# Two-layer transformer on one core: the token lists of the experts found by counting in place of repeated maxima

## The reference, cut to what matters

```python
logits = xf @ router_w.T                       # T x 64
scores = softmax(logits)
topk_w, topk_idx = top_k(scores, 8)
topk_w = topk_w / (topk_w.sum(-1, keepdims=True) + 1e-20)
slot_expert = topk_idx.reshape(-1)
onehot = one_hot(slot_expert, 64)
pos = (cumsum(onehot, axis=0) * onehot).sum(-1) - 1
valid = pos < 128
dest = where(valid, slot_expert * 128 + pos, 64 * 128)
# xb[e, s] = the s-th token that chose expert e; zeros where there is none
hmid = silu(xb[e] @ w_gate[e]) * (xb[e] @ w_up[e])     # 512 -> 192
yb   = hmid @ w_down[e]                                # 192 -> 512
# out[token] += yb[e, s] * topk_w
# recurrence, per batch:
r, f, c = silu(xn @ Wr), sigmoid(xn @ Wf), silu(xn @ Wc)
h = associative_scan over 1024 times of h = f*h + (1-f)*c
y = r * rmsnorm(h, ln_scale) @ Wo
```

## Time and profile before

| | |
|---|---|
| time, median of 3 runs | 3461.34 us (3455.7 to 3472.47) |
| time of the profiled execution | 3456.27 us |
| its span | 3454.1 us |
| granted TensorE clock, mean | 0.960 of 2.4 GHz |
| PE busy | 3128.1 us, 91% |
| DVE busy | 1855.5 us, 54% |
| POOL busy | 1606.5 us, 47% |
| ACT busy | 1257.1 us, 36% |
| moved by DMA | 424.95 MB, mean 123 GB/s |

### The profile page before, as it was taken

One profiled execution on the slowest core, in us unless ns is written; L12 is line 12 of the kernel. 1 busy time (PEld: TensorE's weight loads), 2 busy tenths in 40 slices (PEclk: granted clock), 3 DMA queues, 4 the chain that ended last, 5 costly groups with the idle time before them and its releaser, 6 DMA issues. The chain is left out here.

```text
span 3454.1 us, 45609 instructions
## 1 busy us (share of the span) xinstructions
PE 3128.1 (91%) x16217; PEld 2440.1 (71%) x16217; DVE 1855.5 (54%) x3969; ACT 1257.1 (36%) x2827; POOL 1606.5 (47%) x1410
## 2 busy tenths in 40 slices
PE   5999999899999989999998999999858099999996
PEld 3777777777878777787877778787637067676764
DVE  5455556655555565555566555556528852434431
ACT  3344444334434333433333343343352023232322
POOL 2366657624554653455465244545511154444352
PEclk8999999999999999999999999999889599999998
DMA  6433223352223234211222421221073168787876
GB/s 211 157 114 105 97 89 104 131 170 99 89 86 108 89 106 156 86 62 68 80 87 91 154 73 62 80 92 50 22 251 119 36 181 225 205 213 205 220 206 141
DMA packets 219406, 424.95 MB, mean 123 GB/s; under 512 B 22448, under 2 KB 102960, under 8 KB 217136
## 3 DMA queue, kind: packets, MB, share of 16 engines
q1 hardware_dynamic: 200624, 377.99, 32.7%
q0 software_dynamic: 18560, 44.05, 6.8%
HBM read 311.22 MB, written 110.69 MB: 122 GB/s over the span
## 5 line engine op out<-in xcount | busy, mean ns | idle before, releaser
L776 POOL TENSOR_SCALAR probs<-probs,comb 128x512 f32<-128x512 f32 (+3 forms) x384 | 221.6, 586 | 1018.2 <-DVE comb L725 1018.0
L897 ACT ACTIVATE probs<-score_ps,neg_max 128x640 f32<-128x640 f32 (+7 forms) x512 | 374.4, 738 | 481.5 <-DVE neg_max L731 481.5
L731 DVE TENSOR_REDUCE neg_max<-score_ps 128x2 f32<-128x256 f32 (+7 forms) x256 | 347.2, 1356 | 114.4 <-PE score_ps L1025 113.4
L781 POOL TENSOR_TENSOR probs<-probs 128x512 f32<-128x512 f32 (+3 forms) x384 | 383.9, 1014 | 10.7
L785 POOL TENSOR_TENSOR out_root<-out_root,neg_half 128x16 f32<-128x16 f32 x128 | 372.5, 2911 | 4.8 <-DVE out_root L708 4.8
L820 ACT ACTIVATE attT<-turn_ps 128x512 fp32r<-128x512 f32 (+3 forms) x384 | 189.0, 492 | 470.6 <-PE turn_ps L934 468.3
L633 DVE TENSOR_TENSOR layer_sum<-product_ps,layer_sum 128x512 f32<-128x512 f32 x384 | 262.9, 685 | 30.8 <-PE product_ps L40 24.6
L1022 PE MATMUL score_ps<-keys_all,queries_all 64*128 64x512 f32 (+3 forms) x2304 | 278.0, 364 | 0.0
L620 DVE TENSOR_TENSOR attT<-turn_ps,attT 128x512 fp32r<-128x512 f32 (+3 forms) x384 | 212.7, 554 | 106.6 <-ACT attT L820 103.9
L678 DVE SCALAR_TENSOR_TENSOR hidden<-gate_tanh,product_ps 128x512 f32<-128x512 f32 x128 | 88.0, 688 | 312.7 <-ACT gate_tanh L862 312.7
L1022 PEld LDWEIGHTS score_ps<-keys_all,queries_all 64*128 64x128 f32 x2304 | 187.6, 186 | 67.4 <-issue 31.1
(11 more groups left out here) (253 smaller groups left out, 7293.9 us busy)
## 6 DMA issues: line engine op xcount, KB each, us to landing
w_qk<-weights_split SPq DMA_DIRECT2D x48, 512.0 KB, 4.6
w_gate<-weights_split SPq DMA_DIRECT2D x48, 512.0 KB, 3.3
w_up<-weights_split SPq DMA_DIRECT2D x48, 512.0 KB, 3.6
w_down<-weights_split SPq DMA_DIRECT2D x48, 512.0 KB, 6.8
e_gate_up<-in_w_gate_dram SPq DMA_DIRECT2D x64, 384.0 KB
e_gate_up<-in_w_up_dram SPq DMA_DIRECT2D x64, 384.0 KB
e_down<-in_w_down_dram SPq DMA_DIRECT2D x64, 384.0 KB
values_by_head<-hidden_split SPq DMA_DIRECT2D x32, 512.0 KB, 3.3
```

The source lines that it names most:

```text
L731: dve.tensor_reduce(nmax[:, i % 2, :], score_tile(i % NT), AX.X, ALU.max, negate=True)\
L776: pool.tensor_scalar(PR[:, r, 1, c], PR[:, r, 1, c], comb[:, i % 4:i % 4 + 1], 1.0, ALU.mult, ALU.mult)\
L781: pool.tensor_tensor(PR[:, r, 0, c], PR[:, r, 0, c], PR[:, r, 1, c], ALU.add).then_inc(s_comb, 1)
L897: act.activation(PR[:, i % 2, q, 0:(j + 1) * P], score_tile(j)[:, q, :], ACT.Exp, bias=nmax[:, i % 2, q:q + 1], accum_out=sums[:, i % 16, ...
```

## The change

The keys, draws and merges go. The mask `sel` is kept as 128 tokens x 64 experts x 32 tiles of 128 tokens, in bf16. PE multiplies it by an upper triangle of ones (`cum`, 16 matmuls): for each expert and tile, the running count of chosen tokens. A matmul with `below` gives the count at each tile's start. Four DVE operations (`window`) mark for each expert, tile and slot whether the slot lies in the tile, and how far into it. For each of 16 groups of 4 experts PE then makes (`find`, 8 matmuls) the running count minus that distance, DVE compares it with zero (`near`), and PE counts the tokens ahead by a matmul with ones (`counted`). `slot` is three DVE operations. The 1152-column and 1024-column work is gone from DVE, and the transfer `move` too.

The plan's rules change with it: `cols` of the last batch comes three steps sooner; scans may go into a step in which no routing operation went, also before the experts; the experts start one step after `slot` (two before); weights of expert 0 (gate and up) are loaded after most groups are counted, those of expert 1 after the table is made.

```diff
+    G = P // NTT            # 4
+    NG = E // G             # 16
+    BANKS = 3
+        free = [GU, YP, XP]
...
-                yield ("key", b), 0.9
-                for r in range(6 * (b - 1), min(6 * b, ROUNDS)) if b else ():
-                    yield ("early", r), 2.6
             yield ("zsum",), 2.4
-            for r in range(ROUNDS):
-                yield ("draw", r), 3.0 if r + 1 < ROUNDS else 1.5
-                if r == 3:
-                    yield ("topsum",), 2.4
-                    yield ("den",), 0.8
-            for r in range(ROUNDS):
-                yield ("merge", r), 1.0
-            yield ("slot",), 1.5
+            for q in range(4):
+                yield ("window", q), 1.6
+            yield ("topsum",), 2.4
+            yield ("den",), 0.8
+            for g in range(NG):
+                yield ("near", g), 0.7
+            yield ("slot",), 0.6
...
+                            if k == "sel" and b == batches - 1:
+                                later += [(s + 1, ("cum", 0)), (s + 1, ("cum", 1)), (s + 2, ("cum", 2)), (s + 2, ("cum", 3)),
+                                          (s + 3, ("starts",))]
+                            if k == "window" and b == 3:
+                                for g in range(NG):
+                                    find_at[g] = s + 1 + g // 2
+                                    later.append((find_at[g], ("find", g)))
...
                             if k == "slot":
-                                started = s + 2
-                    if scans and scans[0][0:2] in gates_at and not took and (started is not None or not route):
+                                started = s + 1
+                                later.append((s + 1, ("weights",)))
+                    if scans and scans[0][0:2] in gates_at and not took:
...
-                        if v[0] == "slotturn":
+                        if v == ("counted", NG - 2):
                             sp.wait_ge(s_gst, 16)
                             sp.wait_ge(s_pad, 32)
-                            sp.wait_ge(s_left, 2 * ROUNDS - 1)
+                            sp.wait_ge(s_found, NG - 2)
                             load_gate_up(0)
+                        if v[0] == "weights":
+                            sp.wait_ge(s_slot, 3)
+                            load_down(0)
                             load_gate_up(1)
-                            load_down(0)
...
+                    if kind == "window":
+                        if b == 0:
+                            dve.wait_ge(s_start, 1)
+                            dve.tensor_tensor(past[:, :, :], slot_no.unsqueeze(1).to_broadcast([P, NG, P]),
+                                              start.unsqueeze(2).to_broadcast([P, NG, P]), ALU.subtract).then_inc(s_win, 1)
+                        if b == 1:
+                            dve.wait_ge(s_win, 1)
+                            dve.tensor_tensor(inside[:, :, :], past[:, :, :], count[:, :, P - 1:P].to_broadcast([P, NG, P]),
+                                              ALU.is_lt).then_inc(s_win, 1)
...
+                    if kind == "near":
+                        dve.wait_ge(s_find, b + 1)
+                        if b >= 2:
+                            dve.wait_ge(s_found, b - 1)
+                        dve.tensor_scalar(near[:, b % 2, :], free[b % BANKS][:, :], 0.0, None, ALU.is_le).then_inc(s_near, 1)
...
+                    if v[0] == "find":
+                        g = v[1]
+                        pe.wait_ge(s_win, 4)
+                        if g >= BANKS:
+                            pe.wait_ge(s_near, g - BANKS + 1)
+                        j, rows = g % G, slice(g % G * NTT, (g % G + 1) * NTT)
+                        for i in range(G):
+                            at, dst = g // G * G + i, free[g % BANKS][:, i * P:(i + 1) * P]
+                            pe.matmul(dst, count[rows, at, :], inside[rows, at, :], start=True, stop=False)
+                            ins = pe.matmul(dst, minus[rows, :], past[rows, at, :], start=False, stop=True)
+                        ins.then_inc(s_find, 1)
+                    if v[0] == "counted":
+                        g = v[1]
+                        pe.wait_ge(s_near, g + 1)
+                        if g == 0:
+                            pe.matmul(found, minus[:, :], none[:, :], start=True, stop=False)
+                            for at in range(NG):
+                                pe.matmul(found[:, 2 * G * at:2 * G * (at + 1)], inside[:, at, :], tile_one, start=False, stop=False)
+                        for i in range(G):
+                            e = G * (g // G * G + i) + g % G
+                            ins = pe.matmul(found[:, 2 * e:2 * e + 2], near[:, g % 2, i * P:(i + 1) * P], one_none, start=False,
+                                            stop=(g == NG - 1 and i == G - 1))
+                        ins.then_inc(s_found, 1)
```

More of the change, by code:

```diff
@@ L1303, in schedule @@
                 spent = 0.0
-                items += [v for at, v in later if at <= s]
+                items += sorted([v for at, v in later if at <= s], key=lambda v: v[0] == "find")
                 later = [(at, v) for at, v in later if at > s]
                 while todo and (e is None or spent + todo[0][1] / 2 <= allowed + busy):
-                    if todo[0][0][0] == "due" and todo[0][0][1:] not in done and route:
+                    if todo[0][0][0] == "due" and route:
                         break
@@ L1353, in schedule @@
                         ok = {"top": cols_at.get(b, s) < s,
-                              "key": b in turn_at and turn_at.get(b, s) < s,
                               "zsum": ready.get("exp", s) < s,
-                              "merge": b != 0 or ready.get("moved", s) < s,
+                              "window": ready.get("start", s) < s,
+                              "topsum": ready.get("mask", s) < s,
+                              "near": find_at.get(b, s) < s,
                               "slot": ready.get("slot", s) < s}.get(k, True)
@@ L2025, in item @@
[L2025 to L2027 removed]
+                    if v[0] == "cum":
+                        q = v[1]
+                        pe.wait_ge(s_sel, batches)
+                        if q == 0:
+                            pe.wait_ge(s_whole, 6)
+                            pe.wait_ge(s_rows, 2 * batches)
+                            pe.wait_ge(s_lg, batches)
+                        if q >= BANKS:
+                            pe.wait_ge(s_count, q - BANKS + 1)
+                        for j in range(G):
+                            g = G * q + j
+                            ins = pe.matmul(free[q % BANKS][:, j * P:(j + 1) * P], sel[:, G * g:G * g + G, :].rearrange("p e i -> p (e i)"),
+                                            upto, start=True, stop=True)
+                        ins.then_inc(s_cum, 1)
@@ new lines, in item @@
+                    if v[0] == "starts":
+                        pe.wait_ge(s_count, NG // G)
+                        pe.matmul(start, below, count[:, :, P - 1], start=True, stop=True).then_inc(s_start, 1)
+                    if v[0] == "find":
[9 more added lines that the diff above has]
+                        ins.then_inc(s_find, 1)
```

182 lines of the change are left out of this document (78 added, 104 removed).

## The result

The changed kernel takes 3440.4 us (median of 5 runs, 3437.17 to 3443.2), the kernel before 3460.6 us (5 runs, 3455.7 to 3472.47): ratio 0.9939, interval 0.9918 to 0.9959. It is faster by 20 us. The forecast was 3404, and its range 3380 to 3430 does not hold the time. The profiled execution took 3437.17 us with a span of 3435.0.

What follows compares the result with a forecast made beforehand. PE was taken as the bound: its work plus its standing time. From the profiled 3456.3 us, 106 saved, 16 of new PE work and 38 of new standstills gave 3404 us; range 3380 to 3430.

Steps and rivals of the forecast that it cites:

- The hole: Between batch 1's first turn and expert 0's first matmul: the 105.2 us go but for 4 us of turns, 101 saved.
- The heads: In the last batch's heads, DVE's key and first draw no longer precede the `low` copy PE awaits: 3 us saved.
- PE's new work: 226 added matmuls for counting at 0.08 us, 18 us, less 2 for removed transposes: 16 us (11 to 22).
- windows: PE stands for four DVE operations over 2048 columns between `starts` and `find(0)`: 3 us (1 to 6).
- comparisons: `near(0)` stands behind `topsum`, `den` and a long scan, holding `find(3)` and PE's projection: 3 us (1 to 5).
- expert 0: Small DVE scans ahead of `slot`, then the gather, against two projections of PE work: 3 us (1 to 6).
- Rival 2: Counting is round trips of `find`, `near`, `counted`, uncovered by projections: 34 us for 16 groups, 3438 us; chance 0.12.
- The first expert steps: PE stops: expert 1's weights 6 us (3 to 8), expert 2's turns 5 (3 to 8), expert 3 12 (8 to 15).
- Clock: Low clock after PE's waits, 1.6 us lost each, for some four of the stops: 6 us (2 to 9).
- The end: Last adds into `out`: last `yadd` moves from ahead of expert 59's add to expert 62's; nothing taken.
- Rival 1: PE's stops are shorter than walked, POOL and expert 1's weights being in time: 3378 us; chance 0.17.
- Rivals 3 and 4: 3: round trips with scans in each, slower than before, 0.03. 4: expert steps held by bytes, 3366 us, 0.06.

Runs made afterwards that it cites:

- e6: Changed kernel with every `find` matmul made twice into the same place (128 more); 3451.8 us in one run.
- e7: Changed kernel with spare matmuls ahead of PE's wait in `hidden_turn`, 45 in expert step 3 and 12 in step 33; 3435.9 us.
- e11: Changed kernel with 58 spare matmuls ahead of PE's wait in `hidden_turn(3)` only; 3441.3 us in one run.
- e9: Kernel before the change, with each batch's last four turns moved behind its first projection; 3488.6 us, ratio 1.0080.
- e10: Kernel before the change, with the last four turns behind the batch's first projection and scan groups opened a step later; 3476.9 us, ratio 1.0050.
- e3: Changed kernel with expert 0's down weights and expert 1's gate and up weights issued ahead of expert 2's pair; 3431.8 us, ratio 0.9919.
- e4: Changed kernel with each batch's last four turns moved behind its first projection; 3414.1 us, ratio 0.9866.
- e13: Changed kernel with experts started 13 steps after the table, not one, so remaining projections and turns run ahead of them; 3405.4 us, ratio 0.9843.

## Why the prediction was wrong, point by point

- **The hole** was right. Forecast: first expert at 2675, 92 us sooner; measured 2677.3, 89.8 sooner. Both large waits of the earlier trace rows are gone, and the gather's is 2.4 us.
- **The heads**, 3 us saved: the waits went, the time did not. In the heads alone PE's waits for `t_xT_lo` fell from 5.2 us to 1.4, but the profiled heads took 3.8 us longer; from 2550 to 2600 us the granted clock was 0.80, and 0.97 before.
- **PE's new work** was too dear. In after, `find` matmuls start 0.056 us apart, `counted`'s eight go by in 0.27 us (next rows), and e6 gives 0.045 for a `find` matmul in place. That is some 11 us for the 226, not 18. The Trainium skill (TensorE: Matmul & The Clock Gate, Back-to-back issue gap) has about 81 ns for such a pair, as dear as my 0.08; the `find` matmuls here use 32 rows, and the trace decides.

```profile
2636.50 0.34 PE L2064 MATMUL ht_ps<-whole_numbers,tokens_ahead 128*128 128x2 bf16 x8
2636.77 0.22 PE L2052 MATMUL y_ps<-slot_in_tile,running_count 32*128 32x128 bf16 x1
2636.83 0.21 PE L2053 MATMUL y_ps<-without_top,minus_one 32*128 32x128 bf16 x1
2636.89 0.21 PE L2052 MATMUL y_ps<-slot_in_tile,running_count 32*128 32x128 bf16 x1
```

- **Stops ahead of the experts:** windows 5.0 (forecast 3; next rows), comparisons 1.8 (3), expert 0 3.1 (3, the waits at `xt_ps` and `gu_ps`). Steps of counting 4.6 us (4.7). Rival 2, round trips, is refuted by e6, where doubled PE work lengthens the counting, and by PE's waits for comparisons, six of 0.3 us. That the time lies near its 3438 is a coincidence. The wait for the windows is one operation: the second window took 7.27 us where the first took 2.29, beside POOL's `mask` product. That is 5.0 us more, where the prediction had bounded such a hold by 4.65, and PE had had no work for 5.0 us when `find` began at 2626.89.

```profile
2613.66 2.29 DVE L1677 TENSOR_TENSOR without_top<-whole_numbers,ht_ps 128x2048 bf16<-128x2048 bf16 x1 [0.90 <-PE ht_ps L2043]
2615.47 5.64 POOL L1822 TENSOR_TENSOR route_exp<-route_exp,selected 128x2048 f32<-128x2048 f32 x1
2615.98 7.27 DVE L1681 TENSOR_TENSOR slot_in_tile<-without_top,running_count 128x2048 bf16<-128x2048 bf16 x1
```

- **The first expert steps** were right in sum: 3.8 us at `gu_ps` (6), 4.4 in the turns (5), 13.6 in step 3 (12). Steps 0 to 4 hold 30.1 above PE's work; steps 0 to 3 before hold 2.0. That is 28 against 23 plus 6 of clock.
- **The step that failed** is the one that was left out: "From expert 8 on the steps are about 11 us with PE full", and "nothing else moves after step 51 but single items". I compared what the later steps hold and not in which place of the step it stands. With four projections more in the expert phase, the last cell projection came to the end of the step that opens its scans, and turns bunched in steps without a projection. From step 5 on there is 67.6 above PE's work where the kernel before has, from step 4 on, 33.8: **34 us**. By the table some 13 of them come from scan groups that open, 12 from the turns of batches 2 and 3, 6 in steps 7 and 8 and 4 in the last steps. The prediction named this as its own refutation ("if steps later among the experts grow"), but gave it no term and no rival.
- **Clock**, "some four of the stops above: 6 (2 to 9)": in steps 0 to 4 alone 13.7, in the whole expert phase 32 more than before. Where the stop is a single one, as in step 33, it came to 2.6 us (e7), more than the 1.6 that I had from the earlier trace rows. In step 3 it is not additive (e11).
- **The end**, 0: it gave 6.8 us. Behind the last `yadd` there are two adds of experts and not five as before (one at 3422.54 and four more, at some 5.6 us each):

```profile
3410.20 1.38 POOL L1847 DMA_DIRECT2D out_dram<-rec_out  x1 [3.77 <-DMA out_dram<-e_y,slots]
3420.19 1.66 POOL L1793 DMA_INDIRECT out_dram<-e_y,slots  x1 [8.61 <-DMA out_dram<-rec_out]
3425.80 1.56 POOL L1793 DMA_INDIRECT out_dram<-e_y,slots  x1 [3.95 <-DMA out_dram<-e_y,slots]
```

  The other three now run ahead of it, while PE still works, and the add behind the last `yadd` follows it after 10.0 us, not 13.6.

- **Rival 1** did not come: the stops are longer than walked, not shorter. **Rivals 3 and 4** did not come either: the time is below before's, and the transfers' share among the experts fell to 0.70 where the earlier trace rows have 0.87; the time among the experts grew while they had room. Rival 3 also has a wrong sum: it prices a group against the 34 us of rival 2, but my sum holds 19. With 19 the gain is gone at some 4.5 us a group, not 5.4, and 6 us gives 3481, not 3467.

The forecast was a gain of 52 us, the profiled pair gives 19. Of the 33 missing, 2 lie ahead of the first expert: the heads 7 worse, layer 0 3.5 and PE's new work 7 better. What remains there, some 5 us worse, I put down to the windows (2) and to low clock, 0.93 in 2600 to 2650 us, which lacks 3.5; no run separates these. The rest lies behind it: 34 in the later steps, some 4 in the first ones, less 7 at the end. What stays open: why the heads, on which these edits don't bear, last between 69 and 83 us in the profiles, and whether the sums of e9 and e10 could be forecast at all; I walked single stops rightly there and the totals wrongly.

## What to carry to other kernels

When a change shortens a stage ahead of a planned loop, write down for each later step not only what it holds but in which place, and check each queue for a producer that is now last in the step where its consumer is first. An engine that waits for a queue behind a blocked instruction gains nothing from one reordering if the next thing it needs stands behind the same instruction. If the gain ahead of a loop doesn't reach the end, give the loop its old phase, even at the price of starting it later: here a start 20 us later made the expert phase 71 us shorter, 15 of which are work put ahead of it.

## What the runs showed of the hardware that I had not expected

- A stop of the same length need not lower the clock: in step 49 a wait of 3.5 us left the mean granted clock at 1.00 in after, and in e3 the same wait at the same place gave 0.89.
- The heads' granted clock differs between kernels whose heads are the same: in 2550 to 2600 us it was 0.80 in after and 1.00 in e4, and the heads lasted 76.9 and 69.7 us. A single pair of profiles can differ by that, some 7 us.
- POOL's eight smaller products of `gates` took 3.76 us in e13 with no scan beside them (above), and 9.03 us in step 3 of after, beside DVE's scans; DVE's first scan there took 2.97 us against 1.23 in step 33. The Trainium skill (SBUF — State Buffer, Who interferes with whom) says that only the port pair of DVE and POOL contends, as an exclusive lock; these rows agree, and so does the second window above.

```profile
2737.40 9.03 POOL L1779 TENSOR_TENSOR forget_up<-forget_up 128x512 f32<-128x512 f32 x8
```
